# Top-2 expert tiles: each tile's down products directly behind its own up products, down weights requested one tile sooner, Gelu table loaded ahead

## The reference

```python
normed = _layernorm(hidden_states, rn_g, rn_b)
logits = (jnp.einsum('bld,ed->ble', normed, router_w) + router_b).astype(jnp.float32)
top_w, top_idx = jax.lax.top_k(logits, K)                      # K = 2 of E = 8
top_w = jax.nn.softmax(top_w, axis=-1).astype(hidden_states.dtype)
...
for e in range(E):
    h = _layernorm(hidden_states, ln_g[e], ln_b[e])
    h = jax.nn.gelu(jnp.einsum('bld,di->bli', h, w1[e]) + b1[e], approximate=False)
    h = jnp.einsum('bli,id->bld', h, w2[e]) + b2[e]            # I = 1024 hidden
    out = out + combine[..., e:e + 1] * h
return x + jnp.tanh(g_ffn[1]) * out                            # x: the layer's input
```

## Time and profile before

| | us |
|---|---|
| median of three runs | 733.24 (732.99 to 733.95) |
| the profiled execution | 725.48 |
| its span, first to last instruction | 723.7 |
| PE busy in the span | 668.7 (92%) |
| DVE busy | 367.5 (51%) |
| ACT busy | 315.4 (44%) |
| POOL busy | 359.1 (50%) |

### The profile page before, as it was taken

The page is one execution under the profiler, slowest core; times in us unless marked ns, Lnnn a source line. Parts: engine busy times, 40 slices in busy tenths (PEclk is TensorE's granted clock), DMA queues, the critical chain, the costliest instruction groups (busy, mean ns, idle before and its releaser), DMA issues.

```text
span 723.7 us, 16150 instructions
## 1 busy us (share of the span) xinstructions
PE 668.7 (92%) x5122; PEld 537.5 (74%) x5128; DVE 367.5 (51%) x1131; ACT 315.4 (44%) x847; POOL 359.1 (50%) x566
## 2 busy tenths in 40 slices
PE   4889999999999999998998878999999999999995
PEld 2456666666749999997765535899987899789974
DVE  3578888997568554543887778121113121312220
ACT  3446666666453433322677662423223233232321
POOL 6345555543025755433357782644545455455423
PEclk9999999999999999999999999999999999999998
DMA  6896666661949999923244356679995658364511
GB/s 206 184 200 133 132 135 132 133 118 33 336 131 332 380 375 376 367 86 103 50 77 67 59 194 201 184 214 302 313 273 126 162 141 222 65 164 103 140 31 16
DMA packets 153143, 126.58 MB, mean 175 GB/s; under 512 B 51265, under 2 KB 142700, under 8 KB 153066
## 3 DMA queue, kind: packets, MB, share of 16 engines
q1 hardware_dynamic: 143258, 113.02, 55.0%
q0 software_dynamic: 9808, 12.60, 8.6%
HBM read 163.24 MB, written 23.87 MB: 259 GB/s over the span
## 4 chain that ended last, share of the span: by engine, by line
PE 66%; DVE 11%; DMA 6%; ACT 6%; issue 5%; SPq 4%; POOL 2%; ACTq 0%; DVEq 0%; POOLq 0%
PE e_HP L1300 13%; PE e_Y L1338 12%; PE e_HP L1042 8%; PE e_Y L1054 8%; PE O L692 3%; DVE a_nm L540 3%; ACT a_pexp L396 3%; PE S L1968 2%; PE e_HP L1968 2%; PE S L658 2%; DMA c_flat<-c_att 2%; PE e_Y L1352 1%; PE S L676 1%; PE c_U L2288 1%; DVE a_res L510 1%
## 5 line engine op out<-in xcount | busy, mean ns | idle before, releaser
L1393 ACT ACTIVATE w_down<-e_HP,e_col 128x128 f32<-128x128 f32 x256 | 73.1, 369 | 145.4 <-PE e_HP L1300 145.4
L1300 PEld LDWEIGHTS e_HP<-e_rT,w_up 128*128 128x128 f32 x1024 | 118.6, 192 | 4.5 <-issue 2.2
L1300 PE MATMUL e_HP<-e_rT,w_up 128*128 128x128 f32 x1024 | 120.3, 276 | 1.1 <-ACT e_rT L1379 0.9
L1490 POOL DMA_INDIRECT out<-e_yo,d_table x38 | 61.1, 1608 | 116.5 <-DVE e_yo L1447 83.5
L1338 PE MATMUL e_Y<-w_down 128*128 128x256 f32 x512 | 115.7, 379 | 1.4 <-DMA w_down<-L_ffn_w_in 1.4
L1338 PEld LDWEIGHTS e_Y<-w_down 128*128 128x128 f32 x512 | 94.9, 190 | 13.2 <-DMA w_down<-L_ffn_w_in 1.6
L1444 DVE TENSOR_TENSOR e_yo<-e_Y,e_b2b 128x256 f32<-128x256 f32 x35 | 14.9, 424 | 163.6 <-PE e_Y L1338 142.9
L540 DVE TENSOR_REDUCE a_nm<-S 128x2 f32<-128x512 f32 x128 | 83.0, 682 | 18.2 <-PE S L660 18.2
L396 ACT ACTIVATE a_pexp<-S 128x1024 f32<-128x1024 f32 x64 | 64.0, 1014 | 23.6 <-PE S L680 19.1
L1087 ACT ACTIVATE e_hT<-e_HP,e_col 128x128 f32<-128x128 f32 x128 | 36.5, 369 | 58.2 <-PE e_HP L1042 54.4
L1042 PEld LDWEIGHTS e_HP<-e_rT,w_up 128*128 128x128 f32 x512 | 59.5, 192 | 2.2 <-DVE e_rT L1100 1.5
(11 more groups left out here) (416 smaller groups left out, 1246.4 us busy)
## 6 DMA issues: line engine op xcount, KB each, us to landing
w_up<-L_ffn_w_in SPq DMA_DIRECT2D x38, 1024.0 KB
w_down<-L_ffn_w_in SPq DMA_DIRECT2D x32, 1024.0 KB
w_up<-L_ffn_W_in SPq DMA_DIRECT2D x16, 1024.0 KB, 9.0
w_down<-L_ffn_W_in SPq DMA_DIRECT2D x16, 1024.0 KB, 11.4
scr<-a_parts SPq DMA_DIRECT2D x48, 128.0 KB
e_b2b<-L_ffn_b_in SPq DMA_DIRECT2D x48, 128.0 KB, 7.6
x_sb<-L_ffn_w_in SPq DMA_DIRECT2D x6, 1024.0 KB
ctx_sb<-L_ffn_w_in SPq DMA_DIRECT2D x6, 1024.0 KB
```

What stands on the lines that cost most here:

```text
L1300: m = e.matmul(HP[i % 2][:, j, :], w1[:, s, k, P * j:P * j + P], rT[:, r, k, :], start=(k == 0), stop=(k == 1))
L1393: m = e.activation(hT[:, r, j, :], HP[i % 2][:, j, :], ACT.Gelu, bias=col[:, n % 4, j:j + 1])
L1490: e.indirect_dma_start(outs, at, yo[:, n % YR], None, bounds_check=TOK - 1, oob_is_err=False, compute_op=ALU.add).then_inc(s_os[n % YR], 16)
```

## The change

In the list of SP, the down weights of tile n + 1 instead of those of tile n are requested in iteration n. On PE, down(n) stands directly behind up(n) and turn_rows(n + 2); down(0) stays behind up(1). The down products of the tile ahead of a mixed tile stay behind `up_lanes`, and `down_lanes` stays behind the next up. On ACT, a Gelu of one column is inserted between the two `soon` and the two `rhs` copies.

```diff
                 for n in range(tiles):
                     if mixed_tile(n) is None:
                         weights(SEQ[n] + (WR - 1), False)
-                        weights(SEQ[n] + (WR - 2), True)
+                        weights(SEQ[n] + (WR - 1), True)
                     if n + 2 < tiles:
                         small(n + 2)
...
                 head.tensor(e)
                 turn_rows(0)
-                for n in range(tiles + 1):
-                    if n < tiles and mixed_tile(n) is None:
+                for n in range(tiles):
+                    if mixed_tile(n) is None:
                         up(n)
-                    elif n < tiles:
+                    else:
                         up_lanes(n)
                     if n + 2 < tiles:
                         turn_rows(n + 2)
-                    if n >= 1 and mixed_tile(n - 1) is None:
+                    if mixed_tile(n) is not None:
                         down(n - 1)
-                    elif n >= 1:
+                        turn_hidden(n)
+                        continue
+                    if n == 0:
+                        continue
+                    if n == 1:
+                        down(0)
+                    elif mixed_tile(n - 1) is not None:
                         down_lanes(n - 1)
-                    if n < tiles and mixed_tile(n) is not None:
-                        turn_hidden(n)
+                    if n + 1 == tiles or mixed_tile(n + 1) is None:
+                        down(n)
...
                 for k in range(2):
                     e.wait_ge(s_rs, k + 1)
                     list_scaled(e, soon[k], part, None, s_ss[0])
+                e.activation(t1[:, 11, 0:1], t1[:, 4, 0:1], ACT.Gelu)
                 for k in range(2):
                     e.wait_ge(s_rt, k + 1)
```

## The result

The changed kernel is slower: 747.81 us (median of 4 runs, 745.46 to 749.9) against 733.12 us (4 runs, 732.88 to 733.95) of the kernel before on the same chip. The ratio is 1.0204, with a 95% interval of 1.0166 to 1.0242. That is a loss of 14.7 us where 6.7 were forecast. The sign was right and so was the mechanism at the mixed tiles; a second cost, at plain tiles, had been put at nothing. The size forecast was less than half of the true one, and the time lies outside the range of 736.0 to 743.6.

What follows compares the result with a forecast made beforehand. The prediction took SP's queue, with full transfer engines, as the bound around tile 13. Its terms 3.2 + 2.2 + 1.5 - 0.2 = 6.7 us, added to 733.24, gave 739.9 us, range 736.0 to 743.6.

Steps and rivals of the forecast that it cites:

- The order on PE: Top-2 tiles on PE: same products in another order; down(n) behind up(n) fits Gelu with some 0.5 us to spare, no wait.
- The step of 3.46 us on SP, at mixed tiles: SP's wait ends 3.46 us later, so small loads come late; tiles 13, 23, 32 cost 3.2, 2.2 and 1.5 us.
- That sign: Sign to look for in the profile after: the wait of DVE's lane `evac` on `e_lcol` is longer by 3 us.
- For a plain tile that costs nothing: Plain tiles: loads behind SP's wait move 3.46 us later, but up(n + 2) moves back by the same 3.46 us; cost nothing.
- elsewhere PE works without a gap: PE in the top-2 stage behind the first tiles: no waits except 1.35 us at tile 10 and 0.64 us at tile 13.
- Worth nothing either way: The 1.35 us wait before tile 10's down products may go or stay, worth nothing, since `up_lanes(13)` waits for SP anyhow.
- The three add: Losses at the three mixed tiles add, as PE and SP are late together after each: 3.2 + 2.2 + 1.5 = 6.9 us.
- The end: Last additions after tile 33: its result is ready some 3.8 us sooner, but another addition stands in front; 0.2 us gained.
- The Gelu table: Early Gelu on ACT before the first `rhs` copy: table load ends 1.1 us before the copy is wanted; no cost, no gain.
- transfers bind harder: Rival around tile 10: its weights land late too and SP is held one more megabyte, 9.8 us loss, 743.0 us; chance 0.12.

Runs made afterwards that it cites:

- second profile: Kernel before and changed kernel each run again without edit, on two other chips: 725.93 against 725.46 us, and 736.99 against 724.28 us.
- the two halves: Changed kernel with small loads ahead of the down request only for mixed tiles (736.12 us), or only for plain tiles (730.60 us).
- mixed ahead: Changed kernel with only the mixed tiles' small loads ahead of the down request's wait, plain tiles' behind it: 736.12 us, ratio 1.0176 to the kernel before.
- down request last: Changed kernel with the down request behind the small loads and the lane weights in SP's iteration: 730.87 us, ratio 1.0078 to the kernel before.

## Why the prediction was wrong

**The order on PE.** It was right that the new order has no wait of its own: 0.7 us behind Gelu, once, in the first profile, and none in the second. The order alone does lose 13.3 us, by late weights, but the change brings the request that it needs.

**The step of 3.46 us on SP, at mixed tiles: right mechanism, terms too small in two of three.** Counted from the plain up products ahead of it (so without what PE was late by then), the first lane load goes out 2.7, 4.3 and 3.2 us later than in the kernel before (forecast 3.2, 3.2 and 3.2), and the tiles cost 2.6, 3.9 and 2.7 us (forecast 3.2, 2.2 and 1.5). Why tile 23 is worst is seen in SP's queue. In the kernel before (second profile):

```profile
597.88 0.37 SPq L2584 DMA_DIRECT2D w_down<-L_ffn_w_in  x1
599.06 0.50 SPq L2609 DMA_DIRECT2D e_col<-top_par  x1
...
605.26 0.08 SPq L2584 DMA_DIRECT2D w_down<-L_ffn_w_in  x1
606.24 0.51 SPq L2603 DMA_DIRECT2D e_lcol<-top_par  x1
```

In the changed kernel:

```profile
602.49 0.38 SPq L2590 DMA_DIRECT2D w_up<-L_ffn_w_in  x1
604.38 0.37 SPq L2590 DMA_DIRECT2D w_down<-L_ffn_w_in  x1
605.56 2.11 SPq L2615 DMA_DIRECT2D e_col<-top_par  x1
...
621.09 0.51 SPq L2609 DMA_DIRECT2D e_lcol<-top_par  x1
...
624.82 1.62 SPq L2611 DMA_DIRECT2D e_b2b<-L_ffn_b_in  x1
```

The earlier request puts the up and the down weights of a new expert into one iteration, where they were in two before. The column load right behind them now holds SP 2.11 us instead of 0.50. The forecast looked for such holds around tile 13, where the kernel before had them already, and took tile 23's queue as it was. The lane `evac` of tile 13 idled 10.54 us for its columns against 5.32 in the kernel before (both second profiles), 5.2 us longer where 3 were forecast. That sign was not a clean one: DVE's work ahead of it ended 3.2 us sooner against PE, because the result of down(10) comes a down group earlier in the new order, and only 2.1 of the 5.2 are a later start of `evac` against PE. In tile 32 the first load is late by just the 3.2 forecast; the last bias of the lanes is then held 0.89 instead of 0.32, and by the last lane load SP is 4.0 us behind. By the profile 0.8 of the missing 1.2 us lie there; the rest is open, and that the hold is more than chance there was not tested.

**"For a plain tile that costs nothing": this step failed.** I moved the small loads and the lane weights by 3.46 us and stopped there. But what stands behind them on SP is the next iteration's up request, and behind that the next wait. The trace had the means to see it.

Up weights take long to land when the transfer engines are full: in the kernel before (second profile) those of tile 9 were requested at 505.06 and, by the semaphore events of the trace, landed at 512.87, for products that started at 513.71; those of tile 10 at 512.30 and 520.85, for 520.96. The transfer engines' share was 0.99 and 1.00 in these two stretches; at 0.72 and 0.74 (up weights requested at 632.66 and 662.58) the landing took 5.1 and 4.8 us. The time to spare was 0.8 and 0.1 us. The profile that the forecast had shows the same, 8.0 and 8.7 us to land and 0.7 and 0.1 us to spare. It also has a short wait at up(6), passed over by "elsewhere PE works without a gap", and up(10) starts 0.16 us more than a tile's 7.25 behind up(9):

```profile
494.86 3.81 PE L1300 MATMUL e_HP<-e_rT,w_up 128*128 128x128 f32 x32 [0.21 <-issue]
...
524.08 3.81 PE L1300 MATMUL e_HP<-e_rT,w_up 128*128 128x128 f32 x32
```

The weights of up(6) landed at 494.77. In the changed kernel (second profile):

```profile
514.49 0.37 SPq L2590 DMA_DIRECT2D w_up<-L_ffn_w_in  x1
...
517.61 2.15 SPq L2615 DMA_DIRECT2D e_col<-top_par  x1
...
523.69 0.37 SPq L2590 DMA_DIRECT2D w_up<-L_ffn_w_in  x1
```

These landed at 522.96 and 532.98, and PE's next up groups follow in its timeline:

```profile
523.04 3.81 PE L1300 MATMUL e_HP<-e_rT,w_up 128*128 128x128 f32 x32 [1.59 <-issue]
...
533.07 3.81 PE L1300 MATMUL e_HP<-e_rT,w_up 128*128 128x128 f32 x32 [2.54 <-issue]
```

So "issue" was the landing of the weights, 0.1 us before each start. They took 8.5 and 9.3 us to land, 0.7 us more than the 7.8 and 8.6 of before. The larger part is the request: that of tile 9 came 1.6 us later than the new order allows (60.32 against 55.24 us after the start of up(0), less 3.46), that of tile 10 by 3.6 (69.52 against 62.48). SP could not catch up, since one of its iterations takes 6.9 us without any wait and with both weight requests skipped (507.62 to 514.49), and a tile of PE 7.25.

**"Worth nothing either way" at tile 10.** The wait for the down weights went, and one of 2.5 us for the up weights came in its place, one group earlier. The argument for zero was that `up_lanes(13)` waits for SP anyhow, so delays ahead of it are hidden. That fails, because SP waits for PE in these iterations: a late PE makes SP later by as much, and tile 13 came 2.6 us late on top of the 3.4.

**"The three add"** held: between the mixed tiles 0.2 us changed each time.

**The end.** In the changed kernel's second profile the last two additions on POOL:

```profile
727.63 1.55 POOL L1496 DMA_INDIRECT out<-e_yo,d_table  x1 [1.97 <-DMA out<-e_yo,d_table]
732.32 1.55 POOL L1496 DMA_INDIRECT out<-e_yo,d_table  x1 [3.14 <-DMA out<-e_yo,d_table]
```

The first of them no longer waits for DVE, as it did in the earlier trace rows. From down(34) to the end it is 12.2 us before and 12.0 now. The 0.2 forecast is what came.

**The Gelu table:** no cost that its own run could resolve, and 1.14 us of idle time left behind it in the trace. The Trainium skill's figure for a switch (ScalarE: Activation LUTs, What ACT_TABLE_LOAD costs), about 2.66 us with a drain, isn't seen here: the row has 1.28 us and the next ACTIVATE starts 0.01 us later.

**The sum.** Forecast 3.2 + 2.2 + 1.5 - 0.2 = 6.7. In the second pair of profiles: 3.4 (tiles 9 and 10) + 2.6 + 3.9 + 2.7 + 0.2 + 0.2 + 0.05 = 13.05, beside 12.7 in the medians (736.99 less 724.28) and 14.7 on the first chip. Of the 6.4 us missed, 3.4 are a term left out and 2.3 are sizes at mixed tiles (9.2 less 6.9); the rest is small. The rival "transfers bind harder" had late weights at tile 10 in it, but by more megabytes, and 3.05 us; it would still have been too low. I gave it 0.12 because I took a full share of the transfer engines as a question of bytes, where it was one of when the request goes out.

What stays open: whether putting only the mixed tiles' small loads ahead gains anything (0.9 us by the medians, 2.1 by single profiles), why the two halves gain less than both together, why the weights of tiles 9 and 10 take 0.7 us longer to land, and why the first chip's loss is 2 us larger than the second's.

## What to carry to other kernels

When a wait in an in-order queue moves to a later event, follow everything behind it in that queue, into the next iteration, until the queue has idle time; here an iteration left the queue some 0.35 us to spare (7.25 less 6.9). Read the time to spare of each large load from its landing to its use, not from the absence of a wait: 0.1 us looks the same as 5 us in a list of waits. And requests with much slack go behind the ones with little; whether one has slack is decided by how early it is asked for, since the kernel with small loads first takes 0.15% more than the kernel before with the request a tile sooner, and 2% more without.

## What the runs showed of the hardware

After some of its waits PE ran the next group at half clock: 5.38 us instead of 3.73 for up(10) behind a wait of 2.48, 6.27 instead of 3.62 for down(30) behind 7.64. It is not the length of the wait alone: behind 2.42 (mixed ahead) and 2.32 (down request last) the group took 5.44 and 5.41, but behind 2.54 in the second profile of the change 3.81, and the first products of `up_lanes` behind 2.94 and 3.35 took their usual 0.62. What decides it stays open.

The issue of a small load can hold SP much longer than its usual 0.50 us. In the second profile of the change the column load behind real requests for lane, up and down weights within 5 us was held 2.15, 2.05 and 2.11 us (517.61, 526.78, 605.56); but behind the same three at 494.02 it took 0.50 and the bias load after it 1.44. So a weight request can cost the queue more than its own 0.37, in what follows it.

The medians of the kernel before differed by 1% between chips (733 us on one, 724 to 725 on three others), more than four of the eight edited kernels moved it, so only ratios to the kernel before on the same chip were compared.
